# Second layer of a four-layer cross-attention stack: key copies issued earlier, some PSUM banks emptied by VectorE, side work dealt by another rate, norms that leave halves, six banks for the MLPs

## The reference

```
h  = concat([ctx, x], axis=1)                   # 256 keys per batch
q  = (x @ q_w + q_b)                            # 16 heads of 16
k, v = split(h @ kv_w + kv_b)
attn = softmax(where(mask, q @ k / 16, -inf))
y  = (attn @ v) @ out_w + out_b + x
n  = rmsnorm(y) * postnorm_w                    # eps 1e-6
x  = gelu(n @ w1 + b1) @ w2 + b2 + x            # w1: 256x1024, w2: 1024x256
```

## Time and profile before

| | us |
|---|---|
| median of three runs | 2201.42 |
| the profiled execution, its time | 2199.37 |
| its span on the core | 2197.60 |
| PE busy | 1968.7 (90%) |
| DVE busy | 1073.5 (49%) |
| ACT busy | 966.7 (44%) |
| POOL busy | 689.4 (31%) |

### The profile page before, as it was taken

One profiled execution on the slowest core, in us unless ns is written; L12 is line 12 of the kernel. 1 busy time (PEld: TensorE's weight loads), 2 busy tenths in 40 slices (PEclk: granted clock), 3 DMA queues, 4 the chain that ended last, 5 costly groups with the idle time before them and its releaser, 6 DMA issues.

```text
span 2197.6 us, 39286 instructions
## 1 busy us (share of the span) xinstructions
PE 1968.7 (90%) x16109; PEld 1659.9 (76%) x16109; DVE 1073.5 (49%) x1965; ACT 966.7 (44%) x2563; POOL 689.4 (31%) x803
## 2 busy tenths in 40 slices
PE   7878877788999999999899999999879788878798
PEld 4666666677888888888788888888766666666587
DVE  3444434544444444445454444444363577777743
ACT  3333343333444444434343444444334367666633
POOL 2312222311231423223233241321121267667500
PEclk9999998999999999999999999999989899999899
DMA  3000001100000000000001000000020100000000
GB/s 104 10 2 7 7 2 40 54 1 20 11 30 1 30 11 11 20 1 20 1 20 49 1 30 11 10 1 1 1 88 1 49 1 1 7 2 6 1 12 28
DMA packets 28181, 38.45 MB, mean 17 GB/s; under 512 B 1745, under 2 KB 19809, under 8 KB 28001
## 3 DMA queue, kind: packets, MB, share of 16 engines
q1 hardware_dynamic: 28000, 35.93, 5.1%
HBM read 33.83 MB, written 2.10 MB: 16 GB/s over the span
## 4 chain that ended last, share of the span: by engine, by line
PE 78%; DVE 9%; ACT 7%; issue 3%; POOL 2%; DMA 1%; SPq 0%; DVEq 0%; ACTq 0%; POOLq 0%
PE ps_high L195 40%; PE ps_four L195 7%; PE ps_four L2447 5%; PE ps_four L2467 5%; PE ps_four L2456 3%; PE ps_four L2251 2%; PE ps_high L2343 2%; PE ps_four L2259 1%; ACT l_pt L1621 1%; PE ps_high L2272 1%; PE ps_high L2234 1%; DVE l_sm L2014 1%; PE ps_four L2373 1%; ACT l_pt L1663 1%; PE ps_four L2383 1%
## 5 line engine op out<-in xcount | busy, mean ns | idle before, releaser
L1717 ACT ACTIVATE l_prob<-ps_four,l_mx 128x129 f32<-128x129 f32 x512 | 182.3, 368 | 576.5 <-DVE l_mx L2049 576.4
L1520 POOL TENSOR_TENSOR l_prob<-l_prob,l_mx 128x516 f32<-128x516 f32 x128 | 134.3, 1049 | 750.2 <-DVE l_mx L2056 750.2
L195 PEld LDWEIGHTS ps_high<-l_wo,l_ao 128*128 128x128 f32 x1536 | 199.3, 190 | 17.6 <-DVE l_ao L2068 6.9
L195 PE MATMUL ps_high<-ctxT,l_wk 128*128 128x512 f32 x768 | 211.4, 411 | 0.0
L195 PE MATMUL ps_high<-l_hT,l_wq 128*128 128x512 f32 x768 | 211.4, 411 | 0.0
L195 PE MATMUL ps_high<-l_wo,l_ao 128*128 128x256 f32 x1536 | 205.7, 283 | 5.5 <-DVE l_ao L2068 5.5
L195 PE MATMUL ps_high<-l_wv,ctxT 128*128 128x512 f32 x768 | 202.2, 398 | 1.7 <-ACT l_qT L1698 1.3
L1486 POOL TENSOR_TENSOR l_sm<-l_sm,l_mask 128x1024 f32<-128x1024 f32 x64 | 150.3, 2371 | 119.9 <-DVE l_sm L2014 119.9
L195 PEld LDWEIGHTS ps_high<-l_wv,ctxT 128*128 128x128 f32 x768 | 141.8, 188 | 44.5 <-ACT l_qT L1698 10.1
L2068 DVE SCALAR_TENSOR_TENSOR l_ao<-ps_four,columns,l_ao 128x512 fp32r<-128x512 f32 x128 | 96.1, 751 | 118.9 <-ACT l_ao L1727 118.9
L195 PEld LDWEIGHTS ps_high<-ctxT,l_wk 128*128 128x128 f32 x768 | 136.0, 190 | 23.5
(11 more groups left out here) (283 smaller groups left out, 3881.5 us busy)
## 6 DMA issues: line engine op xcount, KB each, us to landing
l_staging<-in_L_xattn_wv SPq DMA_DIRECT2D x8, 512.0 KB, 3.8
l_staging<-in_L_xattn_wk SPq DMA_DIRECT2D x8, 512.0 KB, 3.8
l_staging<-in_L_xattn_wq SPq DMA_DIRECT2D x8, 512.0 KB, 4.4
l_staging<-in_L_xattn_wo SPq DMA_DIRECT2D x8, 512.0 KB, 3.6
x_tok<-in_x SPq DMA_DIRECT2D x4, 512.0 KB, 7.3
ctx_tok<-in_ctx SPq DMA_DIRECT2D x4, 512.0 KB, 5.5
l_raw_w<-in_L_xattn_mlp_w SPq DMA_DIRECT2D x2, 1024.0 KB, 7.3
l_w<-in_L_xattn_w_fc SPq DMA_DIRECT2D x2, 1024.0 KB, 6.3
```

What stands on the lines that cost most here:

```text
L195: ins = e.matmul(out, a, b, start=start and i == 0, stop=stop and i == 2, skip_group_check=not check)
L1520: e.tensor_tensor(pr[:, :, 0:S + 1], pr[:, :, 0:S + 1], mx[:, 3, :].unsqueeze(2).to_broadcast([P, GB, S + 1]), ALU.mult).then_inc(sem("poo ...
L1717: ins = e.activation(pr.t[:, b, 0:S + 1], banks[b // 2].t[:, (b % 2) * (S + 2):(b % 2) * (S + 2) + S + 1], ACT.Exp, bias=mx[:, 1, b:b + 1] ...
```

## The change

Seven edits, all in L1:

1. `heads(n+1)` is planned behind `maxima(n, 1)` and ahead of `over_v(n-1)`, if the keys of its group have been begun by then; otherwise where it was.
2. `over.n = 0` behind `maxima(n, 0)`: the ring of low banks starts again at bank 0 in each turn.
3. During the last fill of a turn, behind `probs(n, 0)`, a projection's bank (`cols`) is emptied by DVE and not by ACT (`self.evac`). `l1_heads` waits for all six projections of its group one by one.
4. `L1_RATE` goes from (0.7, 1.0, 1.0, 0.9) to (0.7, 0.85, 0.85, 0.85).
5. The norm of L1 leaves halves itself: `norm_tr` writes to a temporary (a slot of the `work` ring), and `norm_split` on DVE (a cast and a subtraction per half of the features) writes `hi` and `lo` to a buffer of its group. `l_mhs`, `mlp_in` and `beside` are gone.
6. The MLPs draw on six banks: 0, 1, 3, 4, 5, 6.
7. `up3` waits for the norm's last split in place of `dve.mhs`.

```diff
-L1_RATE, L1_SLACK = (0.7, 1.0, 1.0, 0.9), 1
+L1_RATE, L1_SLACK = (0.7, 0.85, 0.85, 0.85), 1
...
             if j == 0:
+                over.n = 0
                 for i, slot in enumerate(low):
...
-            pl.slot(hs, "hs", t)
+            pl.slot(hs, "mhs", t)
...
-            h_done[g] = yield from self.norm(t, g, ("ys", g), ("empty", "out32", t, 1), pw, None, True, 1e-6, ("hs", t), rows_done,
-                                             split=False)
-
-        def mlp_in(g):
-            return self.mlp_input(("hs", ("l1", g)), ("l1", g), h_done[g])
+            h_done[g] = yield from self.norm(t, g, ("ys", g), ("empty", "out32", t, 1), pw, None, True, 1e-6, ("mhs", t), rows_done)
...
+            if n + 1 < B and (n + 1) // GB in begun:
+                heads(n + 1)
             if n > 0:
                 while (n - 1) // GB not in ready:
                     next(rest)
...
-            if n + 1 < B:
+            if n + 1 < B and ("l1_heads", n + 1) not in pl.place:
...
             if n < B:
                 probs(n, 0)
+            self.evac = "dve"
             fill(n)
+            self.evac = "act"
         run(rest)
...
-        run(mlp_in(0))
-        self.l1_mlps = [self.within(mlp(g), self.banks(0, 1, 4, 5), self.work, self.st, "dve.norm_xn") for g in range(G)]
+        self.l1_mlps = [self.within(mlp(g), self.banks(0, 1, 3, 4, 5, 6), self.work, self.st, "dve.norm_xn") for g in range(G)]
...
-            if k == FC and beside is not None:
-                yield from beside()
...
+        def cols(p, j):
+            f, bk = pl.info["cols", p, j], use["cols", p, j]
+            if f["by"] != "dve":
+                return
+            dst = use[f["dst_key"]]
+            out = dst.t[:, j] if f["dst"] is None else dst.t[:, j, :, f["dst"], :]
+            q.wait_ge(*pl.event(("full", "cols", p, j)))
+            q.wait_ge(*pl.event(dst.before))
+            e.tensor_scalar(out, bk.t.rearrange("p (b t) -> p b t", b=GB), f["bias"][:, j:j + 1], None, ALU.add).then_inc(
+                bk.slot.empty, 1)
...
-            q.wait_ge(*pl.done("dve.mhs", m, DC - 1))
+            q.wait_ge(*pl.event(f["in_done"]))
```

More of the change, by code:

```diff
@@ L300, in within @@
         while True:
-            here = self.tr, self.misc, self.side, self.work, self.xn, self.st, self.xn_stage
+            here = self.tr, self.misc, self.side, self.work, self.xn, self.ntmp, self.st, self.xn_stage
             self.tr = self.misc = self.side = tr
-            self.work = self.xn = work
+            self.work = self.xn = self.ntmp = work
             self.st, self.xn_stage = st, xn_stage
@@ L309, in within @@
             finally:
-                self.tr, self.misc, self.side, self.work, self.xn, self.st, self.xn_stage = here
+                self.tr, self.misc, self.side, self.work, self.xn, self.ntmp, self.st, self.xn_stage = here
             yield
@@ L1394, in l1_heads @@
             q.wait_ge(sem("dve.const"), 2)
-            q.wait_ge(*pl.event(f["q_done"]))
-            q.wait_ge(*pl.event(f["k_done"]))
+            for projected in f["done"]:
+                q.wait_ge(*pl.event(projected))
             q.wait_ge(*pl.event(qp.before))
@@ L1857, in l1_xT, with norm_tr @@
         def l1_xT(g, c):
-            bk, xs = use["l1_xT", g, c], use["xs", ("l1", g)].t
-            q.wait_ge(*pl.done("act.l1_xT", g, c))
-            e.tensor_tensor(xs[:, 1, c, :], bk.t, f32(xs[:, 0, c, :]), ALU.subtract).then_inc(bk.slot.empty, 1)
+            bk, xs = use["l1_xT", g, c], use["xs", ("l1", g)]
+            if pl.info["l1_xT", g, c]["by"] == "act":
+                q.wait_ge(*pl.done("act.l1_xT", g, c))
+            else:
+                q.wait_ge(*pl.event(("full", "l1_xT", g, c)))
+                q.wait_ge(*pl.event(xs.before))
+                e.tensor_copy(xs.t[:, 0, c, :], bk.t).then_inc(sem("act.l1_xT"), 1)
+                q.wait_ge(*pl.done("act.l1_xT", g, c))
+            e.tensor_tensor(xs.t[:, 1, c, :], bk.t, f32(xs.t[:, 0, c, :]), ALU.subtract).then_inc(bk.slot.empty, 1)
+        def norm_tr(u, c):
+            if pl.info["norm_tr", u, c]["by"] != "dve":
+                return
+            nm, bk, tmp = self.norms[u], use["norm_tr", u, c], use["ntmp", u]
+            q.wait_ge(*pl.event(("full", "norm_tr", u, c)))
+            q.wait_ge(*pl.event(tmp.before))
+            e.tensor_scalar(tmp.t[:].rearrange("p (c t) -> p c t", c=DC)[:, c, :], bk.t, nm["gain"][:, c:c + 1], None,
+                            ALU.mult).then_inc(bk.slot.empty, 1)
+        def cols(p, j):
+            f, bk = pl.info["cols", p, j], use["cols", p, j]
+            if f["by"] != "dve":
+                return
+            dst = use[f["dst_key"]]
[4 more added lines that the diff above has]
+                bk.slot.empty, 1)
         def l1_key_mask(g):
```

45 lines of the change are left out of this document (27 added, 18 removed).

## The result

The changed kernel takes 2193.94 us (median of 20 runs, 2189.45 to 2202.90), the kernel before in the same rounds 2202.33 us (2192.92 to 2206.84). The ratio is 0.9968, with a 95% interval of 0.9957 to 0.9979: 7.0 us faster (4.6 to 9.5), 8.4 us by the medians. Forecast were 20.3 us, and the 2181 us predicted were not reached; the upper end of the range, 2193, was missed by 0.9 us. At 0.3% the change lies within the 0.5% taken as no change, to which I had given 0.13. My own sign of being wrong came too: the attention moved by less than 3 us.

What follows compares the result with a forecast made beforehand. PE was taken to bound both stages, idling in loops of waits. Terms 1.9 + 5.2 + 2.2 + 0 + 0 + 11.0 = 20.3 us took 2199.37, plus 2.05 to the median, to 2181 us; range 2170 to 2193.

Steps and rivals of the forecast that it cites:

- My own sign of being wrong: Attention stage moving by less than 3 or more than 16 us, or up products still waiting.
- Key copies: Attention: copies ahead of the division mostly turn PE's wait into one for ACT; 1.9 us won, bounds 0 and 12.0.
- Banks from 0: Attention fills behind maxima(n,0): a first-pair bank comes free 1.14 us sooner, in five turns; 5.2 us, bounds 0 and 8.1.
- Projections emptied by DVE: End of attention turns: idle DVE empties projection banks sooner than ACT, so maxima(n,0) start earlier; 2.2 us, bounds -1 and 3.5.
- The rate: Attention: turns hold nearly the same PE work, 0.85 mainly makes room for the norm's chain; 0, bounds -2 and 2.
- Halves: Attention: six cast and subtraction pairs, 6.7 us of DVE, hidden in its idle time; cost 0, 6.7 if cover failed.
- MLPs: Gaps between MLPs vanish and up products after two of them regain full speed; 11.0 us, bounds 6.0 and 13.0.
- the pair of halves in front of the last hidden part: First MLP gap: group 3's cast and subtraction on DVE next to POOL, mostly hidden; a delay of 0.75 us.
- the side banks: MLPs: up products first wait for these three up products later, about 4.5 us, when `x_add` is already done.
- the clock goes the other way: Attention: moved idle time puts eleven more units at half clock, 27 us, giving 2208 us; chance 0.04.
- The first rival: Attention: each gain moves PE earlier into a wait for ACT or DVE; 11.0 us remain, 2190.4 us; chance 0.15.

Runs made afterwards that it cites:

- banks_part: The kernel before with one edit, the ring of single banks starting at bank 0 after each first maxima: 2198.12 us, ratio 0.9992.
- mlp_rate_part: The kernel before with the MLPs' edits (norms leave halves, six banks) and the rate of 0.85: 2208.12 us, ratio 1.0026 to the kernel before.
- warm: The changed kernel with six extra matmuls of 128x512, product unused, before the second maxima of seven units: 2183.40 us, ratio 0.9923 to the kernel before.
- five_banks: The changed kernel with MLPs of groups 1 to 3 on banks 0, 1, 4, 5, 6 and L2's first value projections on bank 7: 2189.01 us.
- attention_part: The kernel before with the attention's edits alone (keys early, banks from 0, projections emptied by VectorE, rate 0.85): 2196.96 us, ratio 0.9981.
- warm_tiny: The changed kernel with five-bank MLPs and one extra 64-column matmul before the second maxima of eight units: 2187.56 us, ratio 0.9933 to the kernel before.

## Why the prediction was wrong, step by step

- **Key copies, 1.9 us.** The mechanism was right: the wait turned into one for ACT. In idle time 0.7 us alone, 2.0 in company. On the kernel before, half speed made it a loss of 3.2 in the one profile.
- **Banks from 0, 5.2 us.** 4.6 us in idle time, so well sized; the fills wait 0.46 us for the first reduce instead of 1.58. In the profile of banks_part two thirds went back to the clock.
- **Projections emptied by DVE, 2.2 us.** 1.3 us in idle time. DVE's copy takes 0.75 us (I took 0.69), and the waits left are 0.89 to 1.05 where I said at most 0.9.
- **The rate, 0.** Not settled by itself; in mlp_rate_part, with the halves and without the other edits, it brought 4.0 us more idle time. The three edits run alone add up to 0.7 + 4.6 + 1.3 = 6.6 us of idle time, the four together to 5.5; no run tells whether the rate or the company took the 1.1.
- **Halves, 0.** Right in the changed kernel. As a statement about the edit it was too wide: in the old order the attention was longer with them (7.1 us in one profile, some 3 by the ratio, which does not exclude none). Their own size was wrong as well. Groups of DVE in the attention after:

```profile
L1971 DVE TENSOR_TENSOR l_hs<-l_work,l_hs 128x512 fp32r<-128x512 f32 x6 | 10.8, 1793 | 0.2
L1969 DVE CAST l_hs<-l_work 128x512 fp32r<-128x512 f32 x6 | 3.1, 524 | 0.0
```

  They took 13.9 us of DVE, not 6.7. That is near the 15 us that the prediction worked out from the earlier trace rows beside the rule of the Trainium skill, page "SBUF — State Buffer", section "SBUF: two separate sides" (the shared lock of VectorE and GpSimd), and the trace agrees: the subtraction took 1793 ns on average, 2.7 us at most with POOL at work beside it, and 0.69 us where POOL stood still, as without a neighbour. As that sentence of the prediction said, they were nearly hidden.
- **MLPs, 11.0 us.** The gaps went and the up products ran at speed, 8.5 + 2.4 us (5.02 for 18 matmuls still holds 0.75 too much). The 0.75 for the pair of halves in front of the last hidden part was 0.5 of wait, but 0.9 of half speed behind it. The first step that failed: I took the side banks to be the only ones that an up product could wait for. The line below the change gives L1's last output product the banks 2, 3, 6 and 7, and L2's transposes and projections take 2, 3 and 6, 7 in code that the diff doesn't touch. That cost 2.98 + 0.87 + 1.45 = 5.3 us of waits, and 1.4 us of half speed stood behind them in this profile (in that of warm the same waits had none). A wait of 1.92 us for the first weights fell to 1.20. With bank 3 out of the ring and L2's values off bank 6 in five_banks, the stage won 7.8 us. My reading that no other engine passes half of either stage was off as well, without harm: DVE was busy 61.9 of 119.0 us in the MLPs.
- **The clock.** This is the second step that failed: I put the clock's part in the attention at nothing. I gave 0.04 to "the clock goes the other way", because "the sum of idle time per turn doesn't grow, only its place". Over all turns it shrank by 5.5 us, and the busy time of the same matmuls still rose by 4.0. Half speed came back in turns 7 and 8, where the kernel before had none. And by turns the sentence was wrong, since the wait moved across the start of the turn: from 3.5 to 5.0 us of idle time in turns 8 and 12 and from 7.3 to 9.7 in turn 15, less in turns 7, 11 and 13. How much the clock takes on average is less sure than the 4.0 of this pair, because the profile of the kernel before was a fast one: attention_part wins 4.2 us by its ratio (0.9 to 7.7), where this pair would give it 2.3. By that the clock took some 2 us, not 4. My price for the rival was all or nothing (eleven units, 27 us); in truth it was a partial one and it stood beside the forecast, not against it.
- **The first rival, the attention gives all back, 2190.4.** For the attention that came close: 1.5 us are left. Its reason (waits for ACT or DVE in place of the won ones) holds for 3.8 us at most, since the idle time fell by 5.5 of 9.3; the rest of what is missing is speed. The number 2190.4 needed the full 11.0 us of the MLPs besides, and those weren't there.
- **The sum.** 9.3 became 5.5 (idle) - 4.0 (clock) = 1.5, and 11.0 became 3.6: 5.1 us in the two stages of the pair, 7.0 by the ratio of many runs. Of the 15.2 us that are missing in the pair the MLPs hold 7.4, 5.3 of them the waits for shared banks; the attention holds 7.8, half of it idle time and half speed. What the profiles don't settle is the 2 us between 5.1 and 7.0.

## What to carry to other kernels

Count idle time and speed of TensorE apart: with equal instruction counts, a rise of its busy time at less idle time means that the clock took part of the gain. Profile more than one execution before you price a difference of 2 or 3 us. Where other engines leave TensorE gaps of some 2 us close together, as here, filling one of them with matmuls that nobody needs can be worth more than shortening another; fill them where they delay nothing, and look at every gap of the turn. Before a ring of PSUM banks is widened, list who else draws from the new banks while it runs.

## What the runs showed of the hardware

- In the changed order the half-speed stretches come back in the same turns of every version (changed kernel, attention_part, five_banks: turns 4, 7, 8, 11, 12, 14, 15, apart from the two ends of the stage), 3 to 7 us each, though the attention began at 107.1, 110.3 and 109.5 us. They are part of the schedule there. In the old order the same turns 0 to 6 lost 2.65 us more in one execution than in another, so not every stretch is.
- They follow stretches in which PE was idle for a third to two thirds of the time, in pieces of at most 2.2 us in turns 7 and 8; no single gap was long. In warm_tiny 0.94 and 0.54 us of work in two stretches of 2.5 us came ahead of the fall, in the changed kernel 1.17 and 0.92. But the kernel before had 1.11, 1.96 and 0.86 us in three such stretches of turn 8 and kept its full clock, and waits of 0.78 and 1.39 us there were followed by full speed in one version and half speed in another. Where the limit lies isn't shown.
- Work in a gap, and not an instruction in it, keeps the clock up: six matmuls of 512 columns in eight gaps made the attention 269.5 us, one of 64 columns in each 284.4.
- In the run of warm the attention's half speed fell to its first and last turn and one stretch in turn 4, and the MLPs, whose order was not touched, had none at all: 119.4 instead of 122.4 us at the same idle time (12.9 us). So 3 us of that stage hang on what came before it or on the moment, not on its own order.
